# A fused cross-attention and NF4 feed-forward kernel on one core: three moves in the order of VectorE and ScalarE

## The reference

```python
x = x + xattn(layernorm(x), ctx)     # Q = x Wq^T + bq, K = ctx Wk^T + bk, softmax(Q K^T / 32) ctx
x = x + ffn(layernorm(x))            # (silu(x Wg^T) * (x Wu^T)) Wd^T, hidden width 3584
Wg, Wu, Wd = NF4_CODE[q] * absmax    # one absmax for each block of 64 weights
```

## Time and profile before

| | |
|---|---|
| median of 3 runs | 1920.83 us (1919.8 to 1923.83) |
| profiled execution, its own time | 1919.48 us |
| its span | 1917.5 us |
| PE busy | 1896.5 us, 99% |
| DVE, ACT, POOL busy | 1628.8, 1446.9, 359.6 us |

### The profile page before, as it was taken

One profiled execution on the slowest core, in us unless ns is written; L12 is line 12 of the kernel. 1 busy time (PEld: TensorE's weight loads), 2 busy tenths in 40 slices (PEclk: granted clock), 3 DMA queues, 4 the chain that ended last, 5 costly groups with the idle time before them and its releaser, 6 DMA issues.

```text
span 1917.5 us, 29450 instructions
## 1 busy us (share of the span) xinstructions
PE 1896.5 (99%) x9743; PEld 962.1 (50%) x9743; DVE 1628.8 (85%) x2691; ACT 1446.9 (75%) x2692; POOL 359.6 (19%) x562
## 2 busy tenths in 40 slices
PE   8999999999999999999999999999999999999999
PEld 3487888744444444444444444444444444444444
DVE  8978999869889899898898898898798898896963
ACT  3887776687998988988988988988999999900000
POOL 0023343301111121121111121121123222210110
PEclk9999999999999999999999999999999999999999
DMA  9248999954464564564464465465579999974462
GB/s 356 70 83 188 260 260 278 303 162 127 116 148 125 113 158 125 117 156 126 113 157 119 115 158 122 111 156 140 143 192 223 245 224 227 233 250 135 151 234 85
DMA packets 437352, 326.14 MB, mean 170 GB/s; under 512 B 371648, under 2 KB 371920, under 8 KB 435280
## 3 DMA queue, kind: packets, MB, share of 16 engines
q1 hardware_dynamic: 392992, 170.55, 40.4%
q0 software_dynamic: 44032, 153.65, 24.9%
q10 hardware_dynamic: 176, 0.07, 0.0%
HBM read 154.31 MB, written 82.31 MB: 123 GB/s over the span
## 4 chain that ended last, share of the span: by engine, by line
PE 67%; ACT 13%; DVE 9%; issue 5%; DMA 1%; SPq 0%; POOL 0%; DVEq 0%; ACTq 0%; POOLq 0%
PE ps L2244 39%; PE ps L2287 23%; PE ps L1632 4%; ACT sq L347 4%; ACT sq L343 3%; DVE w L363 1%; ACT halves L415 1%; DMA T<-tail 1%; DVE tail L2397 1%; PE ps L1600 1%; ACT tail L2318 1%; ACT w L347 1%; ACT T L1766 1%; ACT w L343 1%; DVE halves L431 1%
## 5 line engine op out<-in xcount | busy, mean ns | idle before, releaser
L2244 PE MATMUL ps<-T,wS 128*128 128x512 f16 x4704 | 1017.7, 379 | 5.4 <-DVE ps L2352 2.5
L2244 PEld LDWEIGHTS ps<-T,wS 128*128 128x128 f16 x4704 | 459.6, 98 | 560.2 <-issue 6.9
L347 ACT ACTIVATE sq<-sq 128x512 f32<-128x512 f32 x898 | 516.4, 627 | 0.0
L363 DVE SCALAR_TENSOR_TENSOR w<-sq,w 128x512 f32<-128x512 f32 x590 | 415.9, 705 | 116.6 <-ACT sq L347 107.1
L343 ACT ACTIVATE sq<-q 128x512 f32<-128x512 int32 x598 | 363.4, 631 | 49.3 <-DVE w L363 48.7
L2287 PE MATMUL ps<-T,tail 128*128 128x512 f16 x1584 | 346.4, 380 | 3.9 <-DVE tail L2439 2.7
L2287 PEld LDWEIGHTS ps<-T,tail 128*128 128x128 f16 x1584 | 155.1, 98 | 192.6 <-issue 6.3
L431 DVE SCALAR_TENSOR_TENSOR halves<-w,halves 128x512 f16<-128x512 f32 x240 | 163.4, 690 | 6.6 <-ACT halves L415 6.2
L2287 PE MATMUL ps<-T,wS 128*128 128x512 f16 x768 | 168.4, 379 | 0.0
L2192 POOL DMA_DIRECT2D keep_h<-tail x196 | 106.2, 542 | 292.2 <-DVE tail L2397 292.1
L415 ACT CAST halves<-w 128x512 f16<-128x512 f32 x204 | 126.5, 621 | 43.1 <-DVE w L363 31.6
(11 more groups left out here) (238 smaller groups left out, 1858.1 us busy)
## 6 DMA issues: line engine op xcount, KB each, us to landing
keep_h<-tail POOLq DMA_DIRECT2D x196, 256.0 KB, 2.6
tail<-keep_h POOLq DMA_DIRECT2D x66, 512.0 KB, 4.7
wS<-keep_h POOLq DMA_DIRECT2D x32, 512.0 KB, 4.9
q<-in_L_ffn_down_q POOLq DMA_DIRECT2D x56, 256.0 KB, 4.2
T<-in_x SPq DMA_DIRECT2D x13, 1024.0 KB, 8.6
q<-in_L_ffn_up_q POOLq DMA_DIRECT2D x52, 256.0 KB, 3.0
q<-in_L_ffn_gate_q POOLq DMA_DIRECT2D x48, 256.0 KB, 3.3
keep_x<-T SPq DMA_DIRECT2D x38, 256.0 KB, 4.5
```

The costliest lines, as they stand in the source:

```text
L347: nc.scalar.activation(place, place, ACT.Square, bias=b, scale=a).then_inc(un.s_act, 1)
L363: nc.vector.scalar_tensor_tensor(out=out, in0=square_place(un, u, i - 1), scalar=FACTORS[i - 1][1], in1=un.w[:, buf, :], op0=ALU.add, op1= ...
L2244: last = nc.tensor.matmul(ps[:, bank, :], un.wS[:, z % SLOTS, a, kt, :], t.Tp[side][product][:, :, b, kt, :], start=fresh and n == 0, stop ...
```

## The change

Three things move; nothing is added or taken away. (1) In step 1 the splits of step 2's x rows stand two places sooner on ScalarE and on VectorE (in step 0 they stood there already). (2) Between the stages, ScalarE's hi casts of m = 11 and 12 stand ahead of a run of the decode, and VectorE's lo parts of them stand between the four sums. (3) In the last step but one of each down group the decode on VectorE stops four operations short; these follow behind the eight evictions.

```diff
-                if b + 1 in BY_DMA and o in ((2, 3) if b == 0 else (4, 5)):
+                if b + 1 in BY_DMA and o in (2, 3):
                     rows_hi(b + 1, o % 2)
...
         then.copied(act, 4)
-        streams.act.run(HIDDEN_PHASE + 5)
         late_hi(nc, act, t, 11)
         late_hi(nc, act, t, 12)
+        streams.act.run(HIDDEN_PHASE + 5)
         then.copied(act, 5)
...
-                if b + 1 in BY_DMA and g in ((0, 1) if b == 0 else (2, 3)):
+                if b + 1 in BY_DMA and g in (0, 1):
                     rows_lo(b + 1, g % 2)
...
             t_sum(dve, nc.vector.tensor_tensor, t, LAST, n)
+            if n < 2:
+                late_lo(nc, dve, t, 11 + n)
         streams.dve.run(HIDDEN_PHASE + 5)
-        late_lo(nc, dve, t, 11)
-        late_lo(nc, dve, t, 12)
...
             if c < CH_PAIRS - 1:
-                streams.dve.run(DOWN_PHASE + m)
+                streams.dve.run(DOWN_PHASE + m, STEPS - 1 if c == CH_PAIRS - 2 else 0)
```

## The result

The changed kernel takes 1928.39 us, median (1927.83 to 1930.86); the kernel before, beside it, 1920.8 us (1919.8 to 1923.83). The ratio is 1.0032, 95% interval 1.0019 to 1.0045: slower, and 2.8 us above the upper end of my range. The profiled execution took 1928.48 us, its span is 1926.5 us against 1917.5: +9.0.

What follows compares the result with a forecast made beforehand. TensorE is busy 1896.5 of 1917.5 us, so only its idle time can be won. +1.0 + 0.65 - 1.25 = +0.4 us, with one clock fall of 1.45 +1.85: 1922.7 us, range 1919.0 to 1925.6.

Steps and rivals of the forecast that it cites:

- Part 1: Step 2's rows: the context load ends the wait, so the stall grows from 1.04 to 2.0 us, +1.0 us.
- both delays overlap: Before step 2: VectorE's 1.21 us split and ScalarE's 1.07 us cast together move the second L1892 by 1.0 us.
- nearer to 1.60 than to 2.73: Before step 2: argument that a 2.0 us stall keeps the full clock, against the 0.06 case of three falls.
- Part 2: Between the stages: stalls of 1.60 and 0.36 us become one of 2.76 us, +0.65 us, plus 1.45 if the clock falls.
- Part 3: Down groups: four operations behind the evictions, -1.25 us left behind group 2, or +0.2 with the slow clock.
- The 0.6 us: Behind down group 0: the stall left of the 2.73 us once the evictions start 2.29 us sooner.
- Behind it, group 3 ends at 1695.0 ... so 0.5 us is to spare: End of group 3: its first bank is emptied from about 1693.7, so nothing more is lost there.
- The sum: Whole kernel: +0.4 us at full clock, plus 1.45 for one fall, +1.85 us.
- The clock falls at all three stalls: Rival: half clock also behind the 2.0 us stall before step 2, +4.75 us; chance 0.06.
- ScalarE is held longer: Rival, down groups: each microsecond more delays group 2's end, beyond 0.5 us group 3's too; up to +5 us; chance 0.05.

Runs made afterwards that it cites:

- rows_turned_ahead: Kernel before with only the x-row splits sooner, and in step 1 SyncE turning step 2's rows ahead of the context load: 1927.37 us, 1.0030.
- down_only: Kernel before with only the four decode operations put behind each down group's evictions: 1.0002.
- sums_down: Kernel before with VectorE's late halves 11 and 12 behind slot 5's first two factor operations, plus the down-group edit, no h loads held back: 1920.72 us, 1.0009.
- rows_and_late: Kernel before with the x-row splits and the two late forms moved, without the down-group edit: 1924.4 us, 1.0017.
- after_again: The whole change measured a second time against the kernel before: 1925.46 us, 1.0023.
- late_behind_sums: Kernel before with only the late forms moved, VectorE's halves of 11 and 12 behind slot 5's first two factor operations: 1919.78 us, 0.9989.
- sums_down_spaced: As sums_down, but GpSimd's h loads of steps 53 to 56 held back until pieces 52 and 53 are turned; against the kernel before: 1919.76 us, 0.9984.
- after_third: The whole change measured a third time against the kernel before: 1924.46 us, 1.0034.

## Why the prediction was wrong

**Part 1, the mechanism right, the term a little small, one fall missed.** It said +1.0 us, "both delays overlap", a stall of 2.0 us and no fall. Seven executions with both halves of the edit and the context load first waited 1.9 to 2.5 us, mean 2.2; nine without VectorE's half 0.6 to 1.3, mean 1.0: +1.2 us. The delays overlap as it said (0.9 us for my 1.0); what it left out is that the second L1892 itself lasts 0.4 us longer. The step that failed is the clock: I took 2.0 us as "nearer to 1.60 than to 2.73". It fell in four of the seven, for 1.6 us in the one that I split, so about 0.9 us on average. That splits ready earlier gain nothing is shown by rows_turned_ahead: the load, not the split, holds the rows.

**Part 2, right.** It said +0.65 us and a fall of 1.45. The start of VectorE's L1263 is 395.13 in the after trace, 4.18 us later than in the earlier trace rows. Less 4.18, the after rows

```profile
399.33 1.41 DVE L400 TENSOR_TENSOR w<-w 128x512 f32<-128x512 f32 x2
...
404.35 1.29 DVE L1359 TENSOR_TENSOR T<-ps,T 128x512 f16<-128x512 f32 x2 [0.96 <-ACT T L1352]
```

are at 395.15 and 400.17, where I had 395.2 and 400.2; `late_turn(15)` is at 401.01 (401.05) behind 2.85 us (2.76). The fall came in all seven executions with this order, behind 2.8 to 2.9 us. Together, -1.8 + 2.5 + 1.6 = +2.3 us for my 2.1.

**Part 3, the evictions right, the sum wrong.** It said 0.6, 0.5 and 2.5 us behind the groups and no fall: 0.89, 0.43 and 2.55 us, and no fall; the choice on the clock was called nearly even, and in the seven profiles with this order it stayed in five and fell in two. -1.25 us was to be left behind group 2; -0.8 was (5.61 - 6.40). (The 0.6 us was a slip with no weight in the sum: by the prediction's own rows it is 2.73 - 2.29 = 0.44, and five of the nine profiles with this edit show 0.4 to 0.5.) The step that failed is "Behind it, group 3 ends at 1695.0 ... so 0.5 us is to spare". I looked at the one bank that is emptied at the group's end and not at the pieces that group 3 still receives. The decode runs at ScalarE's rate and isn't made faster by moving four operations, so what TensorE gains against it at a group's end it takes from the lead of every later piece. Those last pieces had none to give: the second execution of the kernel before already waits 1.5 us for one. In the profiled execution that was +3.4 us, more than the whole gain.

**The sum.** I had +1.85. With the measured sizes: part 1 +1.2 and 0.9 on average for its clock, part 2 +2.3, part 3 -0.8 and +3.4 give +7.0 us, which the intervals of all three measurements of the whole change hold (1.0032, 1.0023 and 1.0034 are 6.1, 4.4 and 6.5 us). The pieces' share is the least sure: 3.0, 7.1 and 4.7 us in three executions of the changed kernel, the second and third 11.8 and 3.8 us above their medians, but 0.7 us in down_only and none in sums_down with the same distances, and the ratios of rows_and_late and after_again (1.0017, 1.0023) would leave 1 us for all of part 3. So the mechanism at the pieces is shown, 2.1 us of lead lost and the waits that follow, but not that it costs a median execution 3.4 us. Why pieces landed later in the whole change than in down_only, the runs don't show.

**The rivals.** Two came nearest in time, and neither for its reason. "The clock falls at all three stalls" (+4.75): in no profile of the changed kernel did all three fall. "ScalarE is held longer" (+5) named the end of group 3 as a limit, without a price for the pieces. The range was too narrow for a reason of its own: I bounded costs by rows of a single execution, and one more profile of the same kernel would have shown waits that come and go by 1.5 us.

## What to carry to other kernels

When work is put behind something in a stream that feeds a faster engine, what is gained there is lead lost for everything that stream still delivers: list the later deliveries and the slack of each, issue to use, before pricing the gain. An input that is split earlier gains only if nothing else stands between it and its user; follow the queue that moves it. Waits that end with a DMA's landing need a second profile before any of them is used as a bound. Of the kernels here, late_behind_sums (0.9989) and sums_down_spaced (0.9984) are the two that measured below the kernel before, both by little.

## What the runs showed of the hardware

- The clock behind a wait isn't set by the wait's length in this range. Before step 2 it fell behind waits of 2.1, 2.3, 2.3 and 2.5 us and stayed behind 1.9, 2.2 and 2.4 us. At group 2 it stayed behind 2.6 us in four executions and behind 2.8 in another, and fell behind 2.6 us in sums_down (window 0.57) and sums_down_spaced. It stayed, too, behind the 3.0 us for a turned piece in after_again, in a window of 1.00, and fell behind the 2.5 us for the second one in after_third (0.60). Behind 2.7 us at group 0 it fell in the three profiles of the old order that have that wait, and behind 2.8 to 2.9 us at the late transposes in all seven. All eleven waits of 3.2 to 6.1 us from step 2 on had the half clock behind them. The Trainium skill ("TensorE: Matmul & The Clock Gate", Part 1: The HAM clock gate) says that the moment of a switch varies from run to run; the traces agree, with these numbers.
- A turn of one weight piece landed in 3.0 to 15.5 us within one stretch of one execution (after_again). The slow ones lie beside GpSimd's loads of 512 KB; with two pairs of these held back, the two turns that had taken 6.6 to 15.5 us landed in 3.9 to 5.0.
- VectorE's L1892 over 128x1024 took 1.27 to 1.29 us, and 1.68 to 1.75 when it started while GpSimd's L1533 ran (118 cases in 17 profiles). Where it started first, in rows_act_only, L1533 took 1.74 us against a median of 0.77 there.
